# One-hot stage of the routing: id columns on another engine, the table of experts and the softmax shares at another place

## What is computed

```python
# layer 0
logits = xf @ gate_w + gate_b
probs = jax.nn.softmax(logits, axis=-1)
top2_vals, top2_idx = jax.lax.top_k(probs, 2)      # weights: top2_vals
...
# layer 1
probs = jax.nn.softmax(logits, axis=-1)
top_p, top_idx = jax.lax.top_k(probs, TOP_K)
weights = top_p / top_p.sum(axis=-1, keepdims=True)
```

## Time and profile before

| | |
|---|---|
| median of the runs | 1821.03 us |
| span of the profiled execution | 1815.9 us, from the first to the last instruction |
| beside the span | 5.1 us between that span and the median |
| TensorE busy | 1664.2 us, 92% |
| VectorE busy | 929.7 us, 51% |
| ScalarE busy | 953.4 us, 53% |
| GpSimd busy | 351.2 us, 19% |
| granted TensorE clock, mean | 0.973 |
| routing of layer 0, lines 1936 to 2037 | 446.3 to 482.1 us |
| routing of layer 1, lines 1936 to 2037 | 1337.1 to 1372.3 us |

### The profile page before, as it was taken

One profiled execution on the slowest core, in us unless ns is written; L12 is line 12 of the kernel. 1 busy time (PEld: TensorE's weight loads), 2 busy tenths in 40 slices (PEclk: granted clock), 3 DMA queues, 4 the chain that ended last, 5 costly groups with the idle time before them and its releaser, 6 DMA issues.

```text
span 1815.9 us, 41552 instructions
## 1 busy us (share of the span) xinstructions
PE 1664.2 (92%) x13344; PEld 1538.0 (85%) x13345; DVE 929.7 (51%) x2185; ACT 953.4 (53%) x2191; POOL 351.2 (19%) x315
## 2 busy tenths in 40 slices
PE   4799999999799997778989989989988999999998
PEld 3588788778799996657989989989987999999997
DVE  4578868788522221548878868867771111111111
ACT  1133444444333333467989979889834344434433
POOL 2110000000166665310000000000002333333332
PEclk9899999999899998889999999999999999999999
DMA  9990000104388886400000000000185666666664
GB/s 160 107 170 10 9 10 9 38 18 165 123 208 208 208 208 155 150 15 13 14 13 18 9 19 13 9 19 17 46 295 189 174 180 186 181 176 181 190 176 96
DMA packets 85580, 189.95 MB, mean 105 GB/s; under 512 B 13209, under 2 KB 59545, under 8 KB 76665
## 3 DMA queue, kind: packets, MB, share of 16 engines
q1 hardware_dynamic: 53177, 139.39, 23.3%
q0 software_dynamic: 31504, 48.97, 17.3%
q10 hardware_dynamic: 816, 0.53, 0.1%
HBM read 188.98 MB, written 33.11 MB: 122 GB/s over the span
## 4 chain that ended last, share of the span: by engine, by line
PE 51%; DVE 4%; issue 2%; ACT 1%; DMA 1%; DVEq 0%; POOL 0%; ACTq 0%; POOLq 0%
PE bank L1703 23%; PE bank L2187 12%; PE bank L2226 11%; PE bank L663 1%; PE bank L666 1%; PE bank L2194 1%; ACT arena L1427 1%; DMA arena<-qd 1%; DVE arena L1546 0%; DVE arena L1548 0%; PE bank L2088 0%; DVE arena L1464 0%; PE bank L653 0%; DVE X L2022 0%; DVE arena L1470 0%
## 5 line engine op out<-in xcount | busy, mean ns | idle before, releaser
L1703 PE MATMUL bank<-arena 128*128 128x195 bf16 x5408 | 473.6, 249 | 38.3 <-DVE arena L1548 20.2
L1703 PEld LDWEIGHTS bank<-arena 128*128 128x128 fp8e4 x5408 | 468.8, 98 | 43.0 <-issue 41.4
L1427 ACT ACTIVATE arena<-arena,m_row 128x512 fp8e5<-128x512 f32 (+1 forms) x672 | 402.4, 678 | 70.9 <-DVE arena L1548 48.2
L2187 PEld LDWEIGHTS bank<-X,arena 128*128 128x128 f32 x2832 | 335.7, 193 | 10.0 <-issue 3.7
L2187 PE MATMUL bank<-X,arena 128*128 128x128 f32 x2832 | 338.8, 277 | 0.3
L2290 DVE TENSOR_TENSOR arena<-bank,X 128x256 f32<-128x256 f32 x118 | 50.1, 425 | 563.3 <-PE bank L2226 514.3
L1274 PE MATMUL bank<-arena 128*128 (+1 forms) x1352 | 312.5, 386 | 17.3 <-DVE arena L1180 15.0
L2226 PE MATMUL bank<-arena,X 128*128 x1416 | 325.0, 379 | 1.4 <-ACT X L2264 1.4
L1274 PEld LDWEIGHTS bank<-arena 128*128 128x128 f32 x1352 | 252.5, 191 | 58.5 <-issue 23.7
L2226 PEld LDWEIGHTS bank<-arena,X 128*128 128x128 f32 x1416 | 259.9, 190 | 32.4 <-issue 1.9
L1132 ACT ACTIVATE bank<-arena,s_all 128x384 f32<-128x384 f32 (+1 forms) x234 | 133.7, 573 | 187.6 <-DVE arena L1172 183.6
(11 more groups left out here) (240 smaller groups left out, 1336.7 us busy)
## 6 DMA issues: line engine op xcount, KB each, us to landing
arena<-m1w SPq DMA_DIRECT2D x67, 1024.0 KB, 10.8
arena<-m0w SPq DMA_DIRECT2D x67, 512.0 KB
xs<-X SPq DMA_DIRECT2D x4, 1664.0 KB, 6.8
arena<-qd SPq DMA_DIRECT2D x25, 256.0 KB, 3.2
arena<-adjT POOLq DMA_DIRECT2D x13, 448.0 KB, 12.7
arena<-adjT POOLq DMA_DIRECT2D x13, 384.0 KB, 10.8
xe<-zeros POOLq DMA_DIRECT2D x1, 3456.0 KB, 22.0
X<-x_in SPq DMA_DIRECT2D x2, 1664.0 KB, 11.4
```

The source lines that it names most:

```text
L1427: last = a.activation(self.sign[slot].bitcast(F8W)[:, q * W:q * W + nt * P], self.row[r][:, 0:nt * P], ACT.Sigmoid, scale=STEEP, bias=self ...
L1703: last = pe.matmul(bank[rb * NT + n][:, kind * KW:(kind + 1) * KW], self.split[slot][kind].bitcast(F8)[:, q * W + n * P:q * W + (n + 1) * ...
L2187: last = pe.matmul(bank[2 * s + c // 4][:, c % 4 * P:(c % 4 + 1) * P], self.W1[s][:, k * HID + c * P:k * HID + (c + 1) * P], self.rxt[s][: ...
```

## The change

In the one-hot part GpSimd multiplies the id columns, with its own waits; VectorE waits for the readers of `equal` before it writes it and for `hot_used` only before the places; `tile_table()` stands behind the loop. In the picks the shares are made behind both picks and only in layer 0; because the largest logit has then been pushed to about -3e38, its exponential is zero, and 1.0 is added to the sum. `routed` is made ahead of `e2`, and TensorE waits for it alone. A few semaphores of the attention are merged, in a branch of layer 1 that is not taken with these inputs.

```diff
@@ semaphores of the attention and of Experts
-                self.found_done = sem(tag + "found_done")
-                self.top_done = sem(tag + "top_done")
+                self.found_done = sem(tag + "found_done") if H == 1 else None
+                self.top_done = sem(tag + "top_done") if H == 1 else None
...
+                self.SHARES = 1 if second_norm else 2
+                self.hot_places = [sem(f"{tag}hot_places{s}") for s in range(2)]
@@ route_vector, picks
                     if top is self.top1:
 
-                        step(v.tensor_tensor(w3, lg3, spread(top), ALU.subtract))
-                        v.tensor_copy(self.shares, self.work).then_inc(self.picked, 1)
                         step(v.scalar_tensor_tensor(out=self.logits, in0=pick, scalar=-3.0e38, in1=self.logits,
                                                     op0=ALU.mult, op1=ALU.add))
+                v.tensor_tensor(self.routed, self.pick1, self.pick2, ALU.add).then_inc(self.picked, 1)
+                if not self.second_norm:
+                    v.tensor_tensor(self.shares.rearrange("p (t e) -> p t e", e=E), lg3, spread(self.top1),
+                                    ALU.subtract).then_inc(self.picked, 1)
                 v.tensor_tensor(self.e2, self.top2, self.top1, ALU.subtract).then_inc(self.picked, 1)
-                v.tensor_tensor(self.routed, self.pick1, self.pick2, ALU.add).then_inc(self.picked, 1)
@@ weights()
-                    v.wait_ge(self.exps, 2)
+                    v.wait_ge(self.exps, self.SHARES)
...
                         step(v.tensor_reduce(self.sums, self.shares.rearrange("p (t e) -> p t e", e=E), AXX, ALU.add))
+                        step(v.tensor_scalar(self.sums, self.sums, 1.0, None, ALU.add))
@@ one-hot chunks
-                    ids = row_id[:, c % 2 * PAIRS:(c % 2 + 1) * PAIRS]
...
-                    v.wait_ge(self.hot_used[b], c // 2 + 1)
-                    if c < 2:
+                    if c >= 2:
+                        v.wait_ge(self.hot_w[b], c // 2)
+                        v.wait_ge(self.hot_ids[b], c // 2)
+                    else:
                         v.wait_ge(self.xn_stored[b], 16)
...
                     if c == 0:
                         weights()
+                    v.wait_ge(self.hot_used[b], c // 2 + 1)
                     v.tensor_tensor(self.hot_place[b].rearrange("p (q m) -> p q m", m=P),
                                     self.place_no.rearrange("p (o m) -> p o m", o=1).to_broadcast([P, PAIRS, P]),
-                                    over(self.place_of[:, q], P), ALU.is_equal)
-                    v.wait_ge(self.hot_equal[b], c // 2 + 1)
-                    v.tensor_tensor(tiles_[:, :, 0, :], eq, over(ids, G), ALU.mult).then_inc(self.hot_ids[b], 1)
-                    if c == 1:
-                        tile_table()
+                                    over(self.place_of[:, q], P), ALU.is_equal).then_inc(self.hot_places[b], 1)
+                tile_table()
@@ route_scalar
-                a.wait_ge(self.picked, 3)
-                a.activation(self.shares, self.shares, ACT.Exp).then_inc(self.exps, 1)
+                a.wait_ge(self.picked, 1 + self.SHARES)
+                if not self.second_norm:
+                    a.activation(self.shares, self.shares, ACT.Exp).then_inc(self.exps, 1)
...
                     a.wait_ge(self.hot_equal[b], c // 2 + 1)
+                    a.wait_ge(self.hot_used[b], c // 2 + 1)
@@ route_tensor
-                pe.wait_ge(self.picked, 3)
+                pe.wait_ge(self.picked, 1)
...
                 for c in range(4):
+                    pe.wait_ge(self.hot_places[c % 2], c // 2 + 1)
                     pe.wait_ge(self.hot_ids[c % 2], c // 2 + 1)
@@ route_gpsimd, behind the iota
+                G = SLOT_TILES
+                for c in range(4):
+                    b = c % 2
+                    ids = row_id[:, b * PAIRS:(b + 1) * PAIRS]
+                    tiles_ = self.hot_tile[b].rearrange("p (q k g) -> p q k g", q=PAIRS, k=2)
+                    pool.wait_ge(self.hot_used[b], c // 2 + 1)
+                    pool.wait_ge(self.hot_equal[b], c // 2 + 1)
+                    pool.tensor_tensor(tiles_[:, :, 0, :], self.equal[b].rearrange("p (q g) -> p q g", g=G),
+                                       ids.rearrange("p (q o) -> p q o", o=1).to_broadcast([P, PAIRS, G]),
+                                       ALU.mult).then_inc(self.hot_ids[b], 1)
```

More of the change, by code:

```diff
@@ L809, in rows_vector @@
                     v.tensor_reduce(f3[:, h, :], self.cpos.rearrange("p (t h b) -> p h t b", h=H, b=B)[:, h, :, :],
-                                    AXX, ALU.add).then_inc(self.found_done, 1)
-                v.wait_ge(self.found_done, H)
+                                    AXX, ALU.add).then_inc(self.bin_steps, 1)
+                v.wait_ge(self.bin_steps, 4 + H)
                 for h in range(H):
                     v.tensor_scalar(m_row[:, h * T:(h + 1) * T], found[:, h * T:(h + 1) * T], bin_w[:, h:h + 1],
-                                    top_add[:, h:h + 1], ALU.mult, ALU.add).then_inc(self.top_done, 1)
-                v.wait_ge(self.top_done, H)
+                                    top_add[:, h:h + 1], ALU.mult, ALU.add).then_inc(self.bin_steps, 1)
+                v.wait_ge(self.bin_steps, 4 + 2 * H)
                 si = s_all[:, HT:2 * HT]
@@ L1826, in __init__ @@
                 self.rstd_ready = sem(tag + "rstd_ready")
-                self.x_spilled = sem(tag + "x_spilled")
+                self.x_spilled = sem(tag + "x_spilled") if second_norm else None
                 self.lg_done = sem(tag + "lg_done")
@@ L2007, in route_vector @@
                     q, b = slice(c * PAIRS, (c + 1) * PAIRS), c % 2
-                    ids = row_id[:, c % 2 * PAIRS:(c % 2 + 1) * PAIRS]
                     def over(a, n):
                         return a.rearrange("p (q o) -> p q o", o=1).to_broadcast([P, PAIRS, n])
-                    tiles_ = self.hot_tile[b].rearrange("p (q k g) -> p q k g", q=PAIRS, k=2)
-                    v.wait_ge(self.hot_used[b], c // 2 + 1)
-                    if c < 2:
+                    if c >= 2:
+                        v.wait_ge(self.hot_w[b], c // 2)
+                        v.wait_ge(self.hot_ids[b], c // 2)
+                    else:
                         v.wait_ge(self.xn_stored[b], 16)
```

## The result

The changed kernel has a median of 1822.07 us (19 runs, 1818.89 to 1825.87), the kernel before in the same comparisons 1819.69 us (19 runs, 1815.71 to 1823.22). The ratio is 1.0019, with a 95% interval of 1.0012 to 1.0026: 3.4 us slower, 2.2 to 4.7 (the two medians alone differ by 2.4). A second comparison of the same two kernels gave 1.0012 (1.0000 to 1.0023). The forecast was 1823.7 us, 2.7 us over the kernel before.

What follows compares the result with a forecast made beforehand. The routing stages of layers 0 and 1, where TensorE only multiplies fillers and waits, were taken as the bound. Layer 0 +1.03, layer 1 +0.66 and gathers +1.0 gave +2.7 on 1821.03: 1823.7 us, range 1817 to 1828.

Steps and rivals of the forecast that it cites:

- the series of A: One-hot part: VectorE and GpSimd take turns on one way into SBUF, eating the move's gain; the forecast itself, chance 0.48.
- S+22.7 and S+21.7: Forecast ends of the last chunk's products, layers 0 and 1, in us after S, the one-hot part's first comparison.
- the sign of C: Gathers behind one-hot part: late W1 loads hit them, +3.0 layer 1, half in layer 0; sign 5 us landings; chance 0.20.
- Picks, -0.70 in each layer: Routing before the one-hot part: subtract and copy leave VectorE's serial run, routed comes earlier; -0.70 us per layer.
- VectorE and GpSimd as one series: One-hot part: operations reading two SBUF operands exclude each other, making four rounds of 0.87 + 1.81 + 1.9 us.
- the term +1.36: Layer 1's one-hot part: first comparison to the end of products, 21.7 us against 20.34, before the picks' gain.
- Rival D: GpSimd's id products cost more than 1.9 us; 2.15 each gives 1825.4 us; chance 0.10.
- Layer 0, +1.73: Layer 0's one-hot part: 22.7 us against 20.97, first chunk's products at the lower clock, added step hidden under first id product.
- Table late, gathers +1.0 in layer 1 and 0 in layer 0: Expert table behind the last places: later W1 loads share DMA engines with gathers, +1.0 us in layer 1, 0 in layer 0.
- only the first two gathers gate hidden(0) and the loads are then in their second half: Reason given for pricing layer 1's gather delay at 1.0 us, between least 0 and worst 3.0.
- Rival B: One-hot part: GpSimd works beside VectorE unhindered, products end after 19.7 and 17.8 us; 1816.8 us in all; chance 0.17.

Runs made afterwards that it cites:

- e2: Not a run: a value in the kernel's routing code, computed on VectorE in the picks; the change makes routed before it. No measured time or ratio of its own.
- the picks alone: The kernel before with only the picks' edits (routed first, shares behind the picks in layer 0, 1.0 added to the sum); ratio 0.9992 to the kernel before.
- the PSUM constants: The changed kernel with the comparisons' place and tile numbers copied to PSUM ahead of the stage; ratio 1.0009 to the kernel before.
- the versions without exclusion: The changed kernel with comparison constants in PSUM (1.0009); also with first id product behind the weights and table ahead of chunk 2's comparison (0.9954).
- the fastest version: The changed kernel with comparison constants in PSUM, first id product behind the weights, table ahead of chunk 2's comparison; ratio 0.9954 to the kernel before.
- the constants in SBUF: The changed kernel, constants left in SBUF, with table between chunk 2's comparison and places and first id product behind the weights; ratio 0.9982 to the kernel before.
- the table back: The changed kernel with tile_table() back behind chunk 1, all else as changed; ratio 1.0009 to the kernel before.
- the id columns on VectorE: The changed kernel with id products back on VectorE behind the places and table between chunk 2's comparison and places; ratio 0.9976 to the kernel before.
- the table late: The kernel before with tile_table() moved behind the loop and nothing else; ratio 1.0006 to the kernel before.
- the second W1 load behind the gathers: The changed kernel with the second W1 load issued only when the first two gathers have landed; ratio 1.0023 to the kernel before.

## Why the prediction came out right, step by step

The total was right, 2.7 us forecast and 3.4 measured (2.2 to 4.7), and that is in part luck: two of its terms were mis-sized in opposite directions. The two parts came out 2.9 us shorter than forecast (1.96 and 0.97, by the cheaper id product), the gathers 3.6 us dearer (+4.56 in place of +1.0). By the prediction's own signs the series of A is there, but its ends at S+22.7 and S+21.7 came at 21.73 and 19.75, and the first gather of layer 1 landed after more than 5 us, which is the sign of C.

- *Picks, -0.70 in each layer:* -0.67 and -0.70 in the profile, -0.67 and -0.67 in the run of the picks alone. Right.
- *VectorE and GpSimd as one series:* right as a mechanism, shown by the PSUM constants. Its size was off, by GpSimd's price: 1.47 us alone where I took 1.9. Scaling line 546 with an iota's fixed cost was too dear. So was the estimate of 1.80 us from the figure of the Trainium skill (GPSIMD Engine Reference, Performance versus the Vector engine), with 1.47 us measured. Read back from layer 1's times, an id product adds 1.40 us to the series (the series ends at c3's comparison, 13.28 us from S, and 13.28 less 1.03, 5.43 and 2.61 leaves 4.21 for three). Layer 0 gives the same: c3's comparison ends 4.04 us after the start of place(2), and 4.04 less 1.81 and 0.87 is 1.36. With 1.4 in place of 1.9 the forecast's 21.7 becomes 19.7, and the term +1.36 becomes -0.64 (measured 19.75 and -0.60). Rival D, a higher price, is refuted.
- *Layer 0, +1.73:* measured +0.76. The lower clock for c0 came as forecast (4.6 us against 4.7). The added step did not lie hidden under the first id product: it was itself kept out, and reciprocal and multiply came after. My sum had left this out; the weights start 3.30 us from S, in layer 1 without that step 2.77. Against the cheaper id product it cancels, so that c0's buffer is free at S+11.2, forecast 11.1; the rest of the difference, 0.97, is the two id products behind it.
- *Table late, gathers +1.0 in layer 1 and 0 in layer 0:* the mechanism was rightly placed, but the price was rival C's: +3.7 and +0.85. The step that failed is "only the first two gathers gate hidden(0) and the loads are then in their second half". The loads moved from about 1372 to 1379. From the gather's issue at 1373.28 until 1377.00 the trace has 197 DMA packets, all of the hardware queue that carries the loads, and none of the software queue that carries the gathers; from 1377 to 1380 it has 186 of those. So the gather's rows moved only with the end of the loads. In the kernel before, the first gather was issued at 1372.59 and packets of its queue are there from 1374 on. The 2.8 us median, which I held against C, was no guide to this place, and the 5.8 was the row to go by: it is layer 1's fourth gather, issued at 1376.47 beside the 1 MB of b2 (1376.71). Even 5.8 was too low for 6.69. Layer 0's loads, which the forecast had mostly over at S+24, still took 0.87 of the DMA engines from 483 to 484 us, S+24.2 to S+25.2. The landings of the earlier trace rows are all of layer 1, as the trace has none for layer 0's gathers. Why gathers of the tile loop land after 2.8 us beside its W1 loads, no run shows.
- *Rival B*, no exclusion, is refuted as the state of the changed kernel. Its stage for layer 1, 17.8, is not far from what the versions without exclusion reached (18.77 and 18.10).

In sum: +0.09 for layer 0's way to the slots and -1.30 for layer 1's, +4.56 for the gathers, +3.35 us together, beside the measured 3.4; that they agree to a tenth is chance, as the interval is 2.2 to 4.7. The way from hidden(0) to the first gelu adds +1.43 in layer 0 and +0.43 in layer 1, and the profiled spans differ by 4.8. In layer 0 it is b2, slower by more than a microsecond in the changed kernel's profile, as it also is between two profiles of one kernel. In layer 1 it is the products of hidden(0): 64 took 9.08 us in place of 8.65. With late gathers they took 8.96 to 9.62 us, with gathers of 3 us anything from 8.48 to 9.88, so that this belongs to the late gather is not shown.

## What to carry to other kernels

Moving a small piece of work out of a bottleneck also moves the transfers that it releases: ask what else is on the DMA engines at the new time, and price the collision at least by the worst landing in the trace, not the median. Here the gather waited until the loads were nearly through. Before giving VectorE's work to GpSimd, look at both engines' operands: two operands from SBUF in an operation of each made the two engines one here, and a constant in PSUM parted them again. Some small steps with one input are held too (tensor_scalar and cast here), so the fastest version puts them where the other engine is idle.

## What was new about the hardware

- A place comparison on VectorE with one operand in PSUM and one in SBUF runs beside a GpSimd product (1.87 to 1.89 and 1.47 us). With two in SBUF the one that comes second waits: the id product is recorded with 2.99 us under a place comparison, the next comparison with 2.23 in place of 0.95 under the id product.
- One-input steps on 26 or 59 columns were held as well: 1.34 us for tensor_scalar in place of 0.18, 1.37 for the cast. A reduction with one input was not (0.64 us within an id product, with the constants in SBUF and the table at chunk 2; alone it takes 0.63).
- A 1 MB load of b2 landed after 4.8 us in one execution and after 7.0 in another of the same program, and the first gelu waits for it. The low clock, too, fell on layer 0's c0 in some profiles, on c2 of both layers in others (the table back, the picks alone) and on none of the chunks in two (the constants in SBUF, the id columns on VectorE). Differences of a microsecond or two in one profile are no finding unless a wait explains them.
- The first gather of layer 1 took 6.6 to 6.8 us with 2 MB of weight loads issued 2.0 to 2.4 us before it (two profiles of the changed kernel, one of the table late), 5.6 with them issued 3.2 us before it (the constants in PSUM), and 2.9 to 3.0 in every profile where they were issued 9 us or more before it, or only one of the two ahead of it (the second W1 load behind the gathers).
